# Masking the attention steps of two node tiles by one VectorE operation in a graph attention kernel

## What is computed

```python
seq = (x @ W_seq).reshape(N, H, DH)
score1 = einsum('nhd,d->hn', seq, a1)
score2 = einsum('nhd,d->hn', seq, a2)
scores = leaky_relu(score1[:, :, None] + score2[:, None, :], 0.2)
attn = softmax(scores + (1 - adj) * -65500.0)
hidden = einsum('hij,jhd->ihd', attn, seq).reshape(N, 512)
x = layernorm(x + elu(hidden @ W_out + b_out))
```

## Time and profile before

| what | value |
|---|---|
| median of 3 runs | 724.72 us (724.56 to 724.93) |
| the profiled execution's own time | 722.31 us |
| its span | 720.5 us |
| TensorE busy with matmuls | 699.9 us, 97% of the span |
| VectorE busy | 584.8 us, 81% |
| ScalarE busy | 440.7 us, 61% |
| GpSimd busy | 120.0 us, 17% |
| mean granted clock of TensorE | 0.996 of full speed |

### The profile page before, as it was taken

The page is one execution under the profiler, slowest core; times in us unless marked ns, Lnnn a source line. Parts: engine busy times, 40 slices in busy tenths (PEclk is TensorE's granted clock), DMA queues, the critical chain, the costliest instruction groups (busy, mean ns, idle before and its releaser), DMA issues.

```text
span 720.5 us, 22350 instructions
## 1 busy us (share of the span) xinstructions
PE 699.9 (97%) x10059; PEld 583.5 (81%) x10059; DVE 584.8 (81%) x1008; ACT 440.7 (61%) x352; POOL 120.0 (17%) x148
## 2 busy tenths in 40 slices
PE   7999999999999999999999999999999999999995
PEld 5877999899999999999999997444444444888884
DVE  4558999999999999999999983877767554687774
ACT  1578999999899999999999982433333321100000
POOL 1201020000211102113000001565314210011010
PEclk9999999999999999999999999999999999999998
DMA  9994424213533444334111122897129900010101
GB/s 336 416 416 166 139 61 135 84 44 72 87 69 64 70 76 84 67 67 65 54 53 40 48 63 58 151 200 132 44 42 159 150 1 0 1 60 34 55 31 58
DMA packets 33348, 71.18 MB, mean 99 GB/s; under 512 B 3044, under 2 KB 14052, under 8 KB 31076
## 3 DMA queue, kind: packets, MB, share of 16 engines
q1 hardware_dynamic: 24736, 51.64, 20.9%
q0 software_dynamic: 8240, 17.84, 17.0%
q10 hardware_dynamic: 276, 0.26, 0.1%
HBM read 77.86 MB, written 8.65 MB: 120 GB/s over the span
## 4 chain that ended last, share of the span: by engine, by line
PE 66%; ACT 14%; DVE 7%; issue 6%; DMA 4%; SPq 1%; POOL 1%; POOLq 0%; DVEq 0%; ACTq 0%
PE bank L677 19%; PE bank L815 13%; ACT RZ L894 12%; PE bank L787 12%; PE bank L678 10%; PE bank L749 8%; PE bank L757 4%; DVE RZ L1173 2%; DMA RZ<-in_L_gnn_W_seq_dram 2%; DMA RZ<-s_rows_dram 1%; ACT RP L872 1%; DVE RP L1085 1%; DVE RP L1108 1%; DVE RG L1187 1%; SPq L377 1%
## 5 line engine op out<-in xcount | busy, mean ns | idle before, releaser
L677 PE MATMUL bank<-RP,RG 128*128 128x132 f16 (+1 forms) x4096 | 366.4, 222 | 5.8 <-DVE RP L1108 3.1
L677 PEld LDWEIGHTS bank<-RP,RG 128*128 128x128 fp8e4 x4096 | 364.2, 98 | 7.6 <-DVE RP L1108 4.5
L678 PE MATMUL bank<-RP,MT 128*128 128x66 f16 (+1 forms) x4096 | 365.9, 194 | 0.0
L678 PEld LDWEIGHTS bank<-RP,MT 128*128 128x128 fp8e4 x4096 | 364.3, 98 | 0.2
L894 ACT ACTIVATE RZ<-RZ,TAB 128x2048 fp8e4<-128x2048 f32 x167 | 320.6, 1993 | 3.8 <-DMA RZ<-s_rows_dram 3.0
L1183 DVE TENSOR_TENSOR RG<-RZ,MT 128x512 int32<-128x512 int32 x167 | 113.7, 684 | 6.5 <-ACT RZ L894 5.2
L1173 DVE TENSOR_SCALAR RZ<-RZ,TAB 128x2048 int8<-128x2048 f32 x89 | 114.0, 1281 | 2.2 <-DMA RZ<-s_rows_dram 2.2
L1187 DVE TENSOR_TENSOR RG<-RZ,MT 128x512 int32<-128x512 int32 x89 | 61.8, 694 | 0.0
L749 PE MATMUL bank<-RZ 128*128 128x512 f32 x128 | 57.9, 594 | 0.7 <-ACT RZ L930 0.7
L787 PE MATMUL bank<-RG,RP 128*128 128x512 f16 x256 | 55.7, 379 | 0.0
L560 POOL TENSOR_TENSOR rstd<-vps,mhalf 128x1 f32<-128x1 f32 x32 | 25.9, 809 | 152.9 <-DVE vps L1337 152.9
(11 more groups left out here) (156 smaller groups left out, 776.6 us busy)
## 6 DMA issues: line engine op xcount, KB each, us to landing
RG<-in_adj_t_dram SPq DMA_DIRECT2D x16, 1024.0 KB, 8.2
RZ<-s_rows_dram SPq DMA_DIRECT2D x60, 256.0 KB, 3.3
seq_copy_dram<-SEQ SPq DMA_DIRECT2D x8, 528.0 KB, 4.7
RZ<-in_x_dram SPq DMA_DIRECT2D x16, 256.0 KB, 3.7
RP<-in_adj_p_dram POOLq DMA_DIRECT2D x8, 512.0 KB, 8.2
RP<-in_adj_tp_dram POOLq DMA_DIRECT2D x8, 512.0 KB, 12.3
out_dram<-RG SPq DMA_DIRECT2D x16, 256.0 KB, 2.0
RQ<-in_x_t_dram SPq DMA_DIRECT2D x2, 1024.0 KB, 13.6
```

The costliest lines, as they stand in the source:

```text
L677: mm(pb[b][:, c:c + 4 * d], step, both, start=(j == 0 and at == 0), stop=(j == NT - 1), skip_group_check=True)
L678: last = mm(pb[b][:, c:c + 4 * d].rearrange("p (e c d) -> p e c d", e=2, c=2)[:, :, 1, :], mask, edge, start=False, stop=(j == NT - 1), sk ...
```

## The change

Three things change.

1. The tiles that VectorE steps itself in even heads from head 2 on are 0, 3, 6, 9, 12, 15 instead of 1, 4, 6, 9, 12, 14. ScalarE's tiles in even heads are then 1 2, 4 5, 7 8, 10 11, 13 14. Odd heads keep 1, 4, 7, 10, 13 for VectorE, so ScalarE's are 0, 2 3, 5 6, 8 9, 11 12, 14 15. Head 0 is as before.
2. From head 1 on two neighbouring tiles of ScalarE are a pair (`PAIRS`). A pair lies in two neighbouring slots of the Z ring (0 1 or 2 3 in turn), the lone tile 0 of odd heads in a fifth slot. VectorE masks a pair by one AND of 1024 words, at the pair's first tile, after waiting for both steps (`z_ready` of the second) and both slots of G. `ZPREV` names the tile that held a slot before; ScalarE waits for the AND of that tile, which for a pair is the AND of both. Where a pair is followed by a tile of VectorE's own, that tile's `own_step` now goes ahead of the pair's AND.
3. `prep` makes a head's two value products by one operation of 1056 elements instead of two of 528.

```diff
--- before.py
+++ after.py
@@ -50,7 +50,7 @@
     NP = 6
     LAG = 5
     NZ = 4
-    OWN = (1, 4, 6, 9, 12, 14)
+    OWN = (0, 3, 6, 9, 12, 15)
     NBH, WHOLE = 6, 12
     HH = H // 2
     DD = D // 2
@@ -71,7 +71,20 @@
     ACTS = [[j for j in range(NT) if j not in o] for o in OWNS]
     ZBASE = [sum(len(a) for a in ACTS[:h]) for h in range(H + 1)]
     DBASE = [sum(len(o) for o in OWNS[:h]) for h in range(H + 1)]
-    ZTILES = [h * NT + j for h in range(H) for j in ACTS[h]]
+    PAIRS = [[] if h == 0 else [j for j in range(NT - 1) if j in ACTS[h] and j + 1 in ACTS[h]] for h in range(H)]
+    ZSLOT, ZPREV, holder, pairs = {}, {}, {}, 0
+    for h in range(H):
+        for j in ACTS[h]:
+            if h == 0:
+                slot = ACTS[0].index(j) % NZ
+            elif j in PAIRS[h]:
+                slot, pairs = 2 * (pairs % 2), pairs + 1
+            elif j - 1 in PAIRS[h]:
+                slot = ZSLOT[h, j - 1] + 1
+            else:
+                slot = NZ
+            ZSLOT[h, j], ZPREV[h, j] = slot, holder.get(slot)
+            holder[slot] = h * NT + j
     NA = 4
     GT = 4
     NP2 = NT // 2
@@ -105,7 +118,8 @@
         XH = RG[:, :].bitcast(f16).rearrange("p (l t d) -> p l t d", l=2, t=NT)
 
         RZ = sb("RZ", [P, 8192], f32)
-        Z8 = RZ[:, 0:2048].bitcast(f8).rearrange("p (s n) -> p s n", s=NZ)
+        Z8 = [m.bitcast(f8) for m in [RZ[:, q * 512:(q + 1) * 512] for q in range(NZ)] + [RZ[:, 3072:3584]]]
+        ZS32 = RZ[:, 3072:3584].bitcast(i32)
         Z32 = RZ[:, 0:2048].bitcast(i32).rearrange("p (s n) -> p s n", s=NZ)
         ZD = RZ[:, 2048:3072].bitcast(i8).rearrange("p (s n) -> p s n", s=2)
         ZD32 = RZ[:, 2048:3072].bitcast(i32).rearrange("p (s n) -> p s n", s=2)
@@ -886,12 +900,12 @@
 
             def step(h, j):
 
-                u, m = h % 2, ZBASE[h] + ACTS[h].index(j)
+                u = h % 2
                 if j == ACTS[h][0]:
                     s1_row_there(sc, h)
-                if m >= NZ:
-                    sc.wait_ge(g_ready, ZTILES[m - NZ] + 1)
-                A(Z8[:, m % NZ, :], S1B[u], ACT.Relu, bias=SK[:, h, j:j + 1], scale=STEEP, saturate=False).then_inc(z_ready, 1)
+                if ZPREV[h, j] is not None:
+                    sc.wait_ge(g_ready, ZPREV[h, j] + 1)
+                A(Z8[ZSLOT[h, j]], S1B[u], ACT.Relu, bias=SK[:, h, j:j + 1], scale=STEEP, saturate=False).then_inc(z_ready, 1)
 
             for t in range(NT):
                 cast_adj(t)
@@ -1081,9 +1095,8 @@
             def prep(h):
 
                 own.wait(ve)
-                for e, tab in enumerate((EE, FF)):
-                    V.tensor_tensor(V2[:, :, e, :], SEQ[:, :, h, :], tab[:, h, :].unsqueeze(2).broadcast_to([P, NT, DV]),
-                                    ALU.mult).then_inc(v2_ready, 1)
+                V.tensor_tensor(V2[:, :, :, :].rearrange("p t e d -> p e t d"), SEQ[:, :, h, :].unsqueeze(1).broadcast_to([P, 2, NT, DV]),
+                                TAB[:, 2:4, h, :].unsqueeze(3).broadcast_to([P, 2, NT, DV]), ALU.mult).then_inc(v2_ready, 2)
 
             def low_operands(h):
 
@@ -1176,11 +1189,17 @@
                 s = (h * NT + j) % NG
                 if h == 0:
                     ve.wait_ge(adj_cast, NT - NA + 1 + j * NA // NG)
+                if j in PAIRS[h]:
+                    m, z = ZBASE[h] + ACTS[h].index(j), ZSLOT[h, j]
+                    ve.wait_ge(g_used, h * NT + (j + 2))
+                    ve.wait_ge(z_ready, m + 2)
+                    V.tensor_tensor(G32[:, s:s + 2, :], Z32[:, z:z + 2, :], MT32[:, j:j + 2, :], ALU.bitwise_and).then_inc(g_ready, 2)
+                    return
                 ve.wait_ge(g_used, h * NT + (j + 1))
                 if j in ACTS[h]:
-                    m = ZBASE[h] + ACTS[h].index(j)
+                    m, z = ZBASE[h] + ACTS[h].index(j), ZSLOT[h, j]
                     ve.wait_ge(z_ready, m + 1)
-                    V.tensor_tensor(G32[:, s, :], Z32[:, m % NZ, :], MT32[:, j, :], ALU.bitwise_and).then_inc(g_ready, 1)
+                    V.tensor_tensor(G32[:, s, :], ZS32 if z == NZ else Z32[:, z, :], MT32[:, j, :], ALU.bitwise_and).then_inc(g_ready, 1)
                 else:
                     m = DBASE[h] + OWNS[h].index(j)
                     ve.wait_ge(zd_ready, m + 1)
@@ -1189,9 +1208,12 @@
             def att_tile(h, j):
                 if j == 0 and 0 in OWNS[h]:
                     own_step(h, 0)
-                if j + 1 in OWNS[h]:
+                if j + 1 in OWNS[h] and j not in PAIRS[h] and j - 1 not in PAIRS[h]:
                     own_step(h, j + 1)
-                masked(h, j)
+                if j in PAIRS[h] and j + 2 in OWNS[h]:
+                    own_step(h, j + 2)
+                if j - 1 not in PAIRS[h]:
+                    masked(h, j)
                 if h > 0 and j == LOWS_AT[h]:
                     front_sums(h - 1)
                 if h > 0 and j == LOWS_AT[h] + 1:
```

## The result

| | before | after |
|---|---|---|
| median of the runs taken together | 724.64 us (4 runs, 722.73 to 724.93) | 735.45 us (4 runs, 733.03 to 736.63) |
| profiled execution: time, span | 722.31, 720.5 us | 736.63, 734.8 us |

The ratio is 1.0154, 95% interval 1.0137 to 1.0172: slower by 10.8 us. The forecast was 734.0, from 729.5 to 738.0; the measured time lies inside.

The account below looks back on a forecast made before the run. TensorE paces the heads, with VectorE nearly full beside it. The terms sum to +9.3 us, taking the profiled 722.31 to 731.6; with the runs' median 2.4 us above that, 734.0 us, range 729.5 to 738.

Parts of the forecast that it names:

- The release, the deciding term: Odd heads 5 to 15: front sums wait behind pair (5, 6) for ScalarE's step 6; 6 x 1.51 = +9.1 us.
- the 1.3 us that I named as a sign: VectorE idles before the pair's AND at tiles 5 and 6 until ScalarE's step ends, some 1.3 us a time.
- Head 2: Pair (4, 5) delays the front sums, and ScalarE comes late from head 1: +2.4 us, +1.5 if ScalarE catches up.
- The ring's part: Step (1, 2) waits for the AND of head 0's tile 15, moving ScalarE's `front_lows(1)` by 0.87 us.
- Head 1: TensorE's waits for tile 3's mask and the front sums: same VectorE work ahead as before, so 0.
- Head 3: Front sums, already late before, come behind the pair: a stall of 2.04 us instead of 1.82, +0.2 us.
- Even heads: From head 4 on, less VectorE work precedes the front sums: head 4 gains 0.9 us, heads 6 to 14 5 x 0.3.
- The sum: All terms over the heads: 9.1 + 0.2 + 2.4 - 0.9 - 1.5 = +9.3 us.
- rival D: Stalls lower TensorE's clock; as a bound each of 8 costs itself again, 13 us: 747 us; chance 0.02.
- A: VectorE bounded; front sums come earlier and TensorE's 4.2 us of waits go: 720 us, faster; chance 0.05.
- B: A wash: TensorE's cover in odd heads is longer than 3.37 us: 723 to 726 us; chance 0.05.
- C: Slots come free in twos, ScalarE's steps start up to 0.87 us late, five even heads lose that: 738; chance 0.08.

Follow-up runs that it names:

- the kernel with `LOWS_AT` 4: Changed kernel with ScalarE's copy and VectorE's front sums one tile earlier (`LOWS_AT` 4 in odd heads from 3, 3 in head 2): 734.50 us, ratio 1.0159.
- the kernel with the ring alone: Changed kernel with only the ring turned: head 1's first pair in slots 2 and 3 instead of 0 and 1; 732.77 us, ratio 1.0138.

## Why the prediction was right, point by point

**The release, the deciding term.** Confirmed in place, kind and size. The forecast put the pair at T + 2.72, the sums at T + 3.86 and the restart at T + 4.88, a stall of 1.51. Measured are T + 2.85, T + 4.00 and T + 5.02, a stall of 1.65. Nearly all of the 0.14 is one term that I had at nothing: the 0.12 us from the end of ScalarE's step to the start of the AND that waited for it. The pair held VectorE 1.15 us, where I took 1.14 from the slope of other rows. The Trainium skill ("VectorE: DVE Perf Modes", "The DRAIN you can't avoid") would have the next operation start when the first is over, here 1.22, and adds that one that is not held back starts earlier; by the rows it starts 0.07 earlier. VectorE's idle time in front of the pair was smaller than the 1.3 us that I named as a sign: 0.81 in head 5, 16.7 over 17 places. The forecast counted 8 stalls at such places, and there were 8. The order shows the cause: with the sums moved ahead of the AND the loss is gone, and with one mask more ahead of the sums most of it is back in a kernel that has no pairs.

**Head 2.** +2.4 forecast, 2.5 measured. The ring's part was forecast as 0.9 of it; taking it away took 0.8. ScalarE's delay of head 1 came as worked out: the AND of tile 15 is there at 90.69 instead of the earlier trace rows 88.28 and the copy of head 1's sums at 118.72 instead of the forecast 116.35. Both are 2.4 late because in this execution the heads began 2.0 us late and waited longer in head 0: TensorE restarted there at 72.44 us instead of 70.04.

**Head 1.** Forecast as 0, measured 0.1: 0.4 us more for the mask of the pair, 0.3 less for the sums.

**Head 3.** A stall of 2.04 forecast, 2.17 measured.

**Even heads.** Their 0.89 and five of 0.3 are gone, as forecast. This is VectorE's timeline in head 6 of the changed kernel, where ScalarE's copy began at 217.20:

```profile
215.81 1.23 DVE L1196 TENSOR_TENSOR RG<-RZ,MT 128x1024 int32<-128x1024 int32 x1 [0.20 <-ACT RZ L908]
216.95 1.25 DVE L1098 TENSOR_TENSOR RP<-SEQ,TAB 128x1056 f32<-128x1056 f32 x1
218.12 1.04 DVE L1121 TENSOR_TENSOR RP<-RP,bank 128x396 f32<-128x396 f32 x2
```

The sums start at T + 0.92, forecast as T + 1.0.

**The sum.** Forecast +9.3, measured 10.2 for the front sums' waits; eight stalls at 0.11 more on average are the difference. 10.2 on top of the median of before, 724.64, gives 734.8; measured are 735.45. Part of this closeness is luck: the 1.7 us of clock were in no term, and how many of the four executions have them is not known.

**What I gave a chance of 0.02.** The clock (rival D) did fall, at one stall of eight, and cost 1.7 us. I had argued from the 1.82 us stall of the earlier trace rows that the length was harmless, and left out that head 3's would be longer. As a rule for all eight stalls the rival is wrong: behind the 2.53 us in head 2 and the 1.65 us in head 5 the clock stayed at 1.00. The Trainium skill ("TensorE: Matmul & The Clock Gate", "HAM oscillation") tells of a kernel whose clock fell again at every wait between its bursts of matmuls. Those waits were longer than the stalls here, and the eight stalls here brought the clock down once.

**The other rivals.** A (VectorE bounds, the change frees it) falls: VectorE got 3.8 us of work less and the kernel is slower. Its gain exists, though: it is the 1 to 2 us of the pairs with an early release. B (a longer cover) falls with the stalls. C (ScalarE falls behind) is seen in head 1 alone; over the heads ScalarE waited for TensorE 22.0 us instead of 13.1 and so had more room, not less. It came true in two experiments, in which ScalarE's copy moved or its ring was mixed.

## What to carry to other kernels

Merging two operations of an in-order engine moves the first one's end to the second one's input. So ask first what the engine releases right behind the merged operation, and when the second input comes: here 4 us of saved work cost 10 us of TensorE's time. The first remedy to try is the order and not the merge: an operation that releases the bounding engine goes ahead of everything that it doesn't need, here ahead of one AND, one step and the products of the next head, which (with the ring turned) made 0.6% faster out of 1.5% slower. And a release has a place on each engine that makes it; moving both for the sake of one only moved the stall.

## What the runs showed of the hardware that I had not expected

TensorE's granted clock fell to half after a single stall in an otherwise full stretch, and stayed there for about 3.4 us, most of it full work. It did so behind the 2.17 us stall in head 3 of the changed kernel, the 3.4 us stall in head 3 of the kernel with pairs in odd heads only, the 2.58 us stall in head 4 of the kernel with `LOWS_AT` 4, and the 3.6 us stall of the kernel with the sums one mask later, whose stretches of 1 us are these, same columns:

```profile
145.00:146.00 1.00, 0.03 (x1) 0.70 0.25 78
146.00:147.00 1.00, 1.00 (x13) 0.50 0.00 0
147.00:148.00 1.00, 1.00 (x15) 0.50 0.06 16
148.00:149.00 1.00, 1.00 (x17) 0.59 0.00 0
```

It did not after the 1.82 us stall of the earlier trace rows, the 2.53 us of head 2 in the changed kernel, the five of 2.2 us in even heads of the kernel with `LOWS_AT` 4, or the 2.2 us in head 3 of the kernel with the ring alone, whose stretches of 2 us are these:

```profile
144.00:146.00 2.00, 0.28 (x7) 1.00 0.03 10
146.00:148.00 2.00, 1.70 (x39) 1.00 0.38 129
148.00:150.00 2.00, 2.00 (x49) 1.00 0.00 0
```

Stalls of nearly the same length thus went either way, and what decides between them stays open: no run was made for it. Where the clock fell, behind stalls of 2.2 to 3.6 us, it cost 1.4 to 1.7 us each time: half of the 3.4 us, less what of them fell into the stall itself. A sum made from stalls alone leaves this out.
